# Second product of the routed experts: two fp32 matmuls replaced by five fp32r passes over weights and hidden channels split in two parts

## The chip, the cores and the metric

The kernel runs on one core of a Trainium2 chip. The metric is the device time of one execution in microseconds (us). Engines are named as in the profile: PE (TensorE matmul), PEld (its weight loads), DVE (VectorE), ACT (ScalarE), POOL (GpSimd), SP (SyncE, which issues most of the DMAs).

## The reference, cut to what matters

The block is FFN, attention, FFN over 1024 tokens of width 256. Both FFNs use the same weights. The FFN has a shared expert and 16 routed experts of which each token takes four:

```
q_weights, ids = top_k(softmax(x @ gate_w.T), 4)
for each expert e:                      # w13_e: 352 x 256, w2_e: 256 x 176
    h   = silu(x @ w13_e[:176].T) * (x @ w13_e[176:].T)     # 176 hidden channels
    acc = acc + (h @ w2_e.T) * coef_e
out = shared(x) + acc
x   = x + 0.5 * ffn(layernorm(x))       # then attention, then the same FFN again
```

The change concerns `h @ w2_e.T`, the second product, with 176 channels as the contraction.

## The kernel before

Each engine has its own instruction list, written out by hand, and semaphores order them. A layer (an FFN) runs in three stages.

First, norm and router, and 9 of 12 "units" of the shared expert (PE lines 399, 404, 422: fp32 matmuls). Meanwhile POOL scatters rows of the normed tokens to a DRAM area sorted by expert (L853, 32 indirect DMAs a layer), and ACT and DVE split the first expert weights `w13`. ACT copies a float32 weight to fp32r (`WH`, L741) and DVE subtracts that from the weight (`WL`, L966), so `WH + WL` is the weight. `PARTED` says after which unit which experts are split. In the second layer `w13` is loaded again and only `WL` is computed again.

Second, the slots: 47 tiles (`TL`) of 128 token rows, each of one expert whose number is read from a table in SBUF by each engine (`values_load`, TENSOR_LOAD in the trace). An iteration i of the loop holds, on PE: the first product of tile i (L449 to L453, six fp32r passes of 352 columns: hidden token part times WH and WL, lower token part `xl` times WH), the two transposes of the rows of tile i+1 (L434), the second product of tile i-2 (L474, two fp32 matmuls of 256 columns, 88 channels each), and the two transposes of the hidden values of tile i-1 (L461). ACT: silu(i) (L719), the upper part `xt` of tile i+1 (L714), the result of tile i-2 (L725). DVE: row numbers (L1068) and the hidden values `hm` of tile i (L1072), TENSOR_LOAD (L1062), the lower part `xl` of tile i+1 (L1084), a copy `ht` of the transposed hidden values of tile i-1 (L1078). POOL scatters the result rows (L860). Each engine takes its list in that order, and a wait in it holds everything behind it.

Third, the last three shared units, and the gathered result rows are added.

SP issues all input loads in one order: x, constants, shared weights, `w13` in four parts (L313), `W2` (L314), then the slot rows (L332) once all scatters have landed.

## Time and profile before

| | |
|---|---|
| device time, median of 3 runs | 477.45 us (475.16 to 477.74) |
| device time of the profiled execution | 481.29 us |
| its span | 479.5 us |
| PE busy / PEld busy | 440.3 us (92%) / 336.8 us (70%) |
| DVE / ACT / POOL busy | 277.9 (58%) / 168.4 (35%) / 197.9 us (41%) |
| chain of waits, share by engine | PE 82%, DVE 12%, ACT 2%, issue 2% |
| costliest PE group | L474, x376, 97.9 us, mean 382 ns |

Busy time counts overlapping matmuls once. A matmul's own duration is longer than its distance to the next one, since they are pipelined: a cost on PE is read from start to start. Where a list waits on a semaphore, the wait hangs on the next instruction of the list.

### The profile page before, as it was taken

The numbers are of one execution on the slowest core, as the hardware profiler recorded it, in microseconds if no ns is written. First come the engines' busy times: TensorE is split into PE (matmuls) and PEld (weight loads), VectorE is DVE, ScalarE is ACT, GpSimd is POOL, SyncE is SP. The second block draws the span as 40 slices with busy tenths as digits, with TensorE's granted clock in tenths as the row PEclk, the third lists the DMA queues.
The fourth block names the chain that finished last, engine by engine and source line by source line (L and its number), as shares of the span: only waits on it lengthen the run. The fifth ranks groups of instructions, "written<-read, shape, count | busy, mean of one in ns | idle before, by whom it ended". The sixth has DMA issues, their size and how long they took to land.

```text
span 479.5 us, 8311 instructions
## 1 busy us (share of the span) xinstructions
PE 440.3 (92%) x2151; PEld 336.8 (70%) x2151; DVE 277.9 (58%) x801; ACT 168.4 (35%) x466; POOL 197.9 (41%) x207
## 2 busy tenths in 40 slices
PE   6889998999999998989979879899899999999890
PEld 4545567998999995534679755455699899999550
DVE  5664665655665562494876444667565566556237
ACT  3221632444444441227556312010244444444210
POOL 0177720444344443630354107785044444444462
PEclk9988998999999998989989768999999999999895
DMA  7999731344344422900000097322334444442192
GB/s 257 385 390 329 244 111 51 118 126 123 123 124 125 121 81 71 411 1 2 0 0 1 2 333 255 117 86 96 90 118 127 121 126 122 125 122 92 56 350 88
DMA packets 40219, 67.35 MB, mean 140 GB/s; under 512 B 5040, under 2 KB 31408, under 8 KB 40176
## 3 DMA queue, kind: packets, MB, share of 16 engines
q1 hardware_dynamic: 32592, 45.05, 29.2%
q0 software_dynamic: 7584, 21.77, 12.9%
q8 instruction: 21, 0.34, 0.3%
q14 instruction: 22, 0.18, 0.1%
HBM read 41.64 MB, written 25.17 MB: 139 GB/s over the span
## 4 chain that ended last, share of the span: by engine, by line
PE 82%; DVE 12%; ACT 2%; issue 2%; DMA 1%; DVEq 0%; ACTq 0%
PE ps L474 17%; PE ps L399 9%; PE ps L422 8%; PE ps L404 7%; PE ps L453 7%; PE ps L449 7%; PE ps L450 6%; PE ps L434 4%; PE ps L461 4%; PE ps L539 3%; DVE X L1101 2%; PE ps L368 2%; PE ps L620 2%; PE ps L355 1%; DVE WR L1100 1%
## 5 line engine op out<-in xcount | busy, mean ns | idle before, releaser
L860 POOL DMA_INDIRECT rows<-ar,idx x94 | 90.3, 960 | 155.5 <-ACT ar L725 152.7
L474 PE MATMUL ps<-W,ar 88*128 x376 | 97.9, 382 | 2.8 <-DVE ar L1078 2.8
L853 POOL DMA_INDIRECT slots<-XR,pos x64 | 67.5, 1055 | 59.3 <-DVE pos L1026 40.4
L1072 DVE SCALAR_TENSOR_TENSOR ar<-ps,XR,ar 128x176 f32<-128x176 f32 x94 | 37.7, 401 | 84.1 <-ACT ar L719 84.1
L449 PE MATMUL ps<-WH,xt 128*128 x188 | 69.3, 369 | 2.8 <-ACT xt L714 1.5
L474 PEld LDWEIGHTS ps<-W,ar 88*128 88x128 f32 x376 | 63.9, 190 | 9.1 <-issue 3.8
L450 PE MATMUL ps<-WL,xt 128*128 x188 | 61.0, 325 | 0.0
L719 ACT ACTIVATE ar<-ps 128x176 f32<-128x176 f32 x94 | 29.9, 318 | 81.8 <-PE ps L453 81.8
L725 ACT ACTIVATE ar<-ps 128x256 f32<-128x256 f32 x94 | 36.2, 385 | 50.8 <-PE ps L474 50.8
L399 PE MATMUL ps<-XT,WS 128*128 128x512 f32 x96 | 52.8, 679 | 1.0 <-ACT sgt L702 1.0
L422 PE MATMUL ps<-WS,ar 128*128 128x256 f32 (+1 forms) x192 | 46.0, 385 | 4.1 <-DVE ar L954 4.1
L422 PEld LDWEIGHTS ps<-WS,ar 128*128 128x128 f32 (+1 forms) x192 | 36.0, 190 | 19.6 <-issue 9.3
L453 PE MATMUL ps<-WH,xl 128*128 x188 | 46.3, 327 | 0.5 <-DVE xl L1084 0.3
L708 ACT ACTIVATE ar<-ps 128x512 f32<-128x512 f32 (+1 forms) x24 | 14.3, 596 | 86.7 <-PE ps L399 86.7
L1084 DVE TENSOR_TENSOR xl<-ps,xt 128x256 fp32r<-128x256 f32 x94 | 39.9, 424 | 6.9 <-issue 3.1
L1078 DVE COPY ar<-ps 88x256 f32<-88x256 f32 x94 | 39.5, 420 | 3.7 <-PE ps L461 3.7
L714 ACT ACTIVATE xt<-ps 128x256 fp32r<-128x256 f32 x94 | 36.1, 384 | 10.1 <-PE ps L434 10.0
L404 PE MATMUL ps<-XT,WS 128*128 128x512 f32 x80 | 39.4, 616 | 0.0
L449 PEld LDWEIGHTS ps<-WH,xt 128*128 128x128 f32 x188 | 35.6, 189 | 4.4 <-issue 4.4
L461 PE MATMUL ps<-cst,ar 128*88 128x128 f32 x188 | 36.3, 274 | 0.0
L434 PE MATMUL ps<-cst,XR 128*128 128x128 f32 x188 | 36.0, 273 | 0.0
L450 PEld LDWEIGHTS ps<-WL,xt 128*128 128x128 f32 x188 | 36.0, 192 | 0.0
(151 smaller groups left out, 596.4 us busy)
## 6 DMA issues: line engine op xcount, KB each, us to landing
XR<-slots SPq DMA_DIRECT2D x94, 144.0 KB, 2.1
WR<-w SPq DMA_DIRECT2D x8, 1408.0 KB, 14.6
WR<-rows SPq DMA_DIRECT2D x16, 512.0 KB, 7.1
W<-w SPq DMA_DIRECT2D x1, 3072.0 KB, 28.7
slots<-zeros SPq DMA_DIRECT2D x1, 2304.0 KB, 12.8
rows<-ar,idx POOLq DMA_INDIRECT x94
X<-x SPq DMA_DIRECT2D x4, 256.0 KB, 4.3
WS<-wsh SPq DMA_DIRECT2D x2, 512.0 KB, 7.8
```

Of the source, the lines that this page charges most:

```text
L399: mm = pe.matmul(ps[:, 4 + u % 2, :], WS1[:, k, 2 * j, :], XT[:, k, half(h)], start=k == 0, stop=k == KD - 1)
L404: mm = pe.matmul(ps[:, 6 + u % 2, :], WS1[:, k, 2 * j + 1, :], XT[:, k, half(h)], start=k == 0, stop=k == KD - 1)
L422: mm = pe.matmul(ps[:, 2 * h + i // 2, i % 2 * D:(i % 2 + 1) * D], Hs[u % 2][rows, tok(i)], WS2[rows, j, :], start=first and i % 2 == 0, s ...
L434: mm = pe.transpose(ps[:, i % 2, k * P:(k + 1) * P], xs[i % NX][:, k * P:(k + 1) * P], ident)
L449: pe.matmul(to, token, WH[:, bass.ds(e, 1), k, :].rearrange("p a n -> p (a n)"), start=k == 0, stop=False)
L450: pe.matmul(to, token, WL[:, bass.ds(e, 1), k, :].rearrange("p a n -> p (a n)"), start=False, stop=False)
L453: mm = pe.matmul(to, xl[i % 2][:, k * P:(k + 1) * P], WH[:, bass.ds(e, 1), k, :].rearrange("p a n -> p (a n)"), start=False, stop=k == KD - 1)
L461: mm = pe.transpose(ps[0:KE, 6 + i % 2, c * P:(c + 1) * P], hm[i % 2][:, c * KE:(c + 1) * KE], ident)
L474: mm = pe.matmul(ps[:, 2 + i % 2, 0:D], ht[i % 2][:, c * P:(c + 1) * P], w, start=c == 0, stop=c == 1)
L853: pool.indirect_dma_start(out=slots_dram[:, :], out_offset=bass.IndirectOffsetOnAxis(ap=pos[:, t, r:r + 1], axis=0), in_=XR[:, t, :], in_o ...
L860: pool.indirect_dma_start(out=rows_dram[:, :], out_offset=bass.IndirectOffsetOnAxis(ap=idx[:, i:i + 1], axis=0), in_=ys[i % NY], in_offset ...
L1084: dve.tensor_tensor(xl[i % 2], ps[:, i % 2, 0:D], xt[i % 2].bitcast(F32), ALU.subtract).then_inc(s_xl, 1)
```

## The change

The weights of the second product are kept as three fp32r arrays. Of the 176 channels the first 112 (`FM`) are the main part, the last 64 (`FR`) the rest. `MH` and `ML` are the upper and lower part of the main weights (112 partitions). `RH` holds the upper part of the rest in partitions 0 to 63 and its lower part in 64 to 127. DVE writes the hidden values with the rest twice (a tile of 112 + 64 + 64), so that the second transpose has the rest in both halves of the partitions. ACT makes the upper part `hh` of the transposed values, DVE the lower part `hl`, and PE makes five fp32r passes: hh x MH, hh x ML, hh x RH (upper and lower weights at once), hl x MH, hl x RH (upper only). The arrays are made once, in the first layer's units 2, 3 (rest) and 7, 8 (main). The rest is loaded twice ahead of `w13`; the main weights are loaded into the same buffer once the rest is split. The DMA descriptor scratch per partition is set to 2048 bytes.

```
-PARTED = {3: (0, 2), ... 8: (14, NE)}
+W2_FIRST = {2: (0, 8), 3: (8, NE)}
+W2_LAST = {7: (0, 4), 8: (4, NE)}
 # SP
+            for b in range(2):
+                sp.dma_start(MR[b * FR:(b + 1) * FR, :, :], w2r).then_inc(s_w2r, 16)
             for e in range(0, NE, 4):
                 sp.dma_start(WR[:, e:e + 4, :, :], w13[e:e + 4]...)
-            sp.dma_start(W2[:, :, :, :], w2.rearrange("e c p n -> p e c n")).then_inc(s_w2, 16)
+            sp.wait_ge(s_rl, len(W2_FIRST))
+            sp.wait_ge(s_rh, len(W2_FIRST))
+            sp.dma_start(MR[0:FM, :, :], w2m).then_inc(s_w2m, 16)
 # PE, slot_hidden
-                wait(pe, s_htc, TL * f + i - 1)
-                for c in range(2):
-                    mm = pe.transpose(ps[0:KE, 6 + i % 2, c * P:(c + 1) * P], hm[i % 2][:, c * KE:(c + 1) * KE], ident)
+                wait(pe, s_hl, TL * f + i - 1)
+                pe.transpose(ps[0:FM, 6 + i % 2, 0:P], hm[i % 2][:, 0:FM], ident)
+                pe.transpose(ps[:, 6 + i % 2, P:2 * P], hm[i % 2][:, FM:FM + P], ident).then_inc(s_ht, 1)
 # PE, slot_out
-                pe.wait_ge(s_htc, TL * f + i + 1)
-                for c in range(2):
-                    w = W2[0:KE, bass.ds(e, 1), c, :]...
-                    mm = pe.matmul(ps[:, 2 + i % 2, 0:D], ht[i % 2][:, c * P:(c + 1) * P], w, start=c == 0, stop=c == 1)
+                pe.wait_ge(s_hh, TL * f + i + 1)
+                pe.matmul(to, hh[i % 2][main, 0:P], of(MH, main), start=True, stop=False)
+                pe.matmul(to, hh[i % 2][main, 0:P], of(ML, main), start=False, stop=False)
+                pe.matmul(to, hh[i % 2][:, P:2 * P], of(RH, slice(0, P)), start=False, stop=False)
+                pe.wait_ge(s_hl, TL * f + i + 1)
+                pe.matmul(to, hl[i % 2][main, 0:P], of(MH, main), start=False, stop=False)
+                pe.matmul(to, hl[i % 2][rest, P:2 * P], of(RH, rest), start=False, stop=True).then_inc(s_l2, 1)
 # ACT, slots: last of an iteration
+                def hidden(i):
+                    act.wait_ge(s_ht, TL * f + i + 1)
+                    wait(act, s_l2, TL * f + i - 1)
+                    act.activation(hh[i % 2], ps[:, 6 + i % 2, 0:D], ACT.Copy).then_inc(s_hh, 1)
 # ACT, part(u), ahead of the WH copies
+                if u in W2_FIRST:
+                    act.activation(RH[:, some, :], MR[:, some, :], ACT.Copy).then_inc(s_rh, 1)
+                if u in W2_LAST:
+                    act.activation(MH[:, some, :], MR[0:FM, some, :], ACT.Copy).then_inc(s_mh, 1)
 # DVE, part(f, u), first layer, ahead of the WL subtractions
+                    dve.tensor_tensor(RH[FR:P, some, :], MR[FR:P, some, :], RH[FR:P, some, :]..., ALU.subtract)
+                    dve.tensor_tensor(ML[:, some, :], MR[0:FM, some, :], MH[:, some, :]..., ALU.subtract)
 # DVE, slots
-                    dve.scalar_tensor_tensor(hm[i % 2], ps[:, 4 + i % 2, FE:2 * FE], row[:, bass.ds(e + R_CF, 1)], sg[i % 2], ...)
+                    dve.scalar_tensor_tensor(hm[i % 2][:, 0:FM], ps[:, 4 + i % 2, FE:FE + FM], rate, sg[i % 2][:, 0:FM], ...)
+                    twice = hm[i % 2][:, FM:FM + 2 * FR].rearrange("p (a n) -> p a n", a=2)
+                    dve.scalar_tensor_tensor(twice, spread(ps[:, 4 + i % 2, FE + FM:2 * FE], 1, 2), rate, spread(sg[i % 2][:, FM:FE], 1, 2), ...)
-                    dve.tensor_copy(ht[i % 2], ps[0:KE, 6 + i % 2, 0:D]).then_inc(s_htc, 1)
+                    dve.tensor_tensor(hl[i % 2][0:FM, :], ps[0:FM, 6 + i % 2, 0:D], hh[i % 2][0:FM, :]..., ALU.subtract).then_inc(s_hl, 1)
-    nc = bacc.Bacc("TRN2", target_bir_lowering=False, num_devices=1)
+    nc = bacc.Bacc("TRN2", target_bir_lowering=False, num_devices=1, dynamic_dma_scratch_size=2048)
```

(`PARTED` itself stays as it was.)

On PE, in the first iteration of the slots that has all four parts, before: the second row transpose, the second product (`W` is the array W2, `ar` holds ht), then the hidden transposes.

```order
L434 MATMUL ps<-cst,XR 128x128
L474 ISA [waits s_htc,s_xsh,s_w2]
L474 MATMUL ps<-W,ar 128x256
L474 ISA
L474 MATMUL ps<-W,ar 128x256
L478 TENSOR_LOAD tab
L461 MATMUL ps<-cst,ar 88x128 [waits s_hm]
L461 MATMUL ps<-cst,ar 88x128
```

The same place now:

```order
L449 MATMUL ps<-cst,XR 128x128
L492 ISA [waits s_hh,s_xsh,s_ml]
L492 MATMUL ps<-MH,hh 128x256
L493 REGISTER_ALU
L493 MATMUL ps<-ML,hh 128x256
L494 REGISTER_ALU
L494 MATMUL ps<-RH,hh 128x256
L496 MATMUL ps<-MH,hl 128x256 [waits s_hl]
L497 MATMUL ps<-RH,hl 128x256
L500 TENSOR_LOAD tab
L475 MATMUL ps<-cst,ar 112x128 [waits s_hm]
L476 MATMUL ps<-cst,ar 128x128
```

Two matmuls became five with two waits among them, where one wait on the copy stood; nothing else changed its place on PE.

On DVE, one iteration of the slots before (`idx` row numbers, `ar` first hm and then ht):

```order
L1068 ISA [waits s_xs3]
L1068 SCALAR_TENSOR_TENSOR idx<-XR,valid,spare 128x1
L1072 ISA [waits s_ht,s_sil]
L1072 SCALAR_TENSOR_TENSOR ar<-ps,XR,ar 128x176
L1062 TENSOR_LOAD tab
L1084 TENSOR_TENSOR xl<-ps,xt 128x256 [waits s_l1,s_xtc]
L1078 COPY ar<-ps 88x256 [waits s_l2,s_ht]
```

and now:

```order
L1112 ISA [waits s_xs3]
L1112 SCALAR_TENSOR_TENSOR idx<-XR,valid,spare 128x1
L1117 ISA [waits s_ht,s_sil]
L1117 SCALAR_TENSOR_TENSOR ar<-ps,XR,ar 128x112
L1121 SCALAR_TENSOR_TENSOR ar<-ps,XR,ar 128x128
L1106 TENSOR_LOAD tab
L1134 TENSOR_TENSOR xl<-ps,xt 128x256 [waits s_l1,s_xtc]
L1127 TENSOR_TENSOR hl<-ps,hh 112x256 [waits s_l2,s_hh]
```

A second SCALAR_TENSOR_TENSOR stands between the silu's wait and the subtraction `xl`, and the copy became a subtraction that waits for ACT in place of PE.

## Rows read from the trace of the kernel before

**Rows 1.** Busy time by engine, clock and DMA in the slots of the first layer.

```profile
core 0: us, PE busy (x) PEld busy (x) DVE busy (x) ACT busy (x) POOL busy (x), PEclk, DMA share, GB/s
90.00:180.00 90.00, 89.91 (x554) 81.97 (x553) 53.16 (x159) 38.95 (x119) 37.45 (x39) 1.00 0.39 117
```

**Rows 2.** Timeline of PE, one steady iteration: start us, us, engine, line, tiles.

```profile
152.92 0.49 PE L453 MATMUL ps<-WH,xl 128*128 x2
...
155.04 0.32 PE L450 MATMUL ps<-WL,xt 128*128 x1
155.20 0.48 PE L453 MATMUL ps<-WH,xl 128*128 x2
155.52 0.38 PE L434 MATMUL ps<-cst,XR 128*128 128x128 f32 x2
155.73 1.03 PE L474 MATMUL ps<-W,ar 88*128 x4
156.60 0.38 PE L461 MATMUL ps<-cst,ar 128*88 128x128 f32 x2
```

**Rows 3.** Timeline, second layer, tiles 1 to 2, where no second product stands yet.

```profile
343.53 0.30 PEld L453 LDWEIGHTS ps<-WH,xl 128*128 128x128 f32 x2
343.64 0.48 PE L453 MATMUL ps<-WH,xl 128*128 x2
...
344.09 0.21 PEld L461 LDWEIGHTS ps<-cst,ar 128*88 128x88 f32 x2
344.16 0.32 ACT L719 ACTIVATE ar<-ps 128x176 f32<-128x176 f32 x1 [1.41 <-PE ps L453]
...
344.62 0.40 DVE L1072 SCALAR_TENSOR_TENSOR ar<-ps,XR,ar 128x176 f32<-128x176 f32 x1 [1.01 <-ACT ar L719]
...
344.90 0.42 PE L449 MATMUL ps<-WH,xt 128*128 x1 [0.34 <-ACT xt L714]
...
345.06 0.42 DVE L1084 TENSOR_TENSOR xl<-ps,xt 128x256 fp32r<-128x256 f32 x1
...
345.54 0.30 PEld L453 LDWEIGHTS ps<-WH,xl 128*128 128x128 f32 x2
345.64 0.49 PE L453 MATMUL ps<-WH,xl 128*128 x2
```

**Rows 4.** The table reads of DVE's and PE's sequencers: duration ns min/median/max.

```profile
L1062 DVEq TENSOR_LOAD <-tab x94: 299/306/570, 73.0 to 444.8; - x94
```

```profile
L478 PEldq TENSOR_LOAD <-tab x94: 295/301/529, 69.7 to 444.2; - x94
```

**Rows 5.** Groups by line: busy us, mean ns of one, idle before it.

```profile
L1072 DVE SCALAR_TENSOR_TENSOR ar<-ps,XR,ar 128x176 f32<-128x176 f32 x94 | 37.7, 401 | 84.1 <-ACT ar L719 84.1
...
L1173 DVE SCALAR_TENSOR_TENSOR U<-U,G,ps 128x128 f32<-128x128 f32 x12 | 3.6, 340 | 0.0
```

**Rows 6.** Timeline of DVE in attention: two such instructions, back to back.

```profile
246.42 0.60 DVE L1173 SCALAR_TENSOR_TENSOR U<-U,G,ps 128x128 f32<-128x128 f32 x2
```

**Rows 7.** Timeline of DVE in the first layer's unit 3.

```profile
44.38 0.69 DVE L954 TENSOR_TENSOR ar<-ps,ar 128x512 f32<-128x512 f32 x1 [2.54 <-PE ps L404]
```

**Rows 8.** Timeline of ACT and DVE, first layer, from unit 8 to the slots.

```profile
67.58 1.46 ACT L741 ACTIVATE WH<-WR 128x704 fp32r<-128x704 f32 x2
```

```profile
69.47 1.68 DVE L966 TENSOR_TENSOR WL<-WR,WH 128x704 fp32r<-128x704 f32 x2
72.26 1.66 DVE L969 SCALAR_TENSOR_TENSOR X<-ps,gate,X 128x256 f32<-128x256 f32 x4 [1.10 <-PE ps L422]
73.83 0.41 DVE L1084 TENSOR_TENSOR xl<-ps,xt 128x256 fp32r<-128x256 f32 x1
```

**Rows 9.** Timeline of PE at the end of the first layer's slots.

```profile
180.18 0.49 PE L453 MATMUL ps<-WH,xl 128*128 x2
...
184.51 1.65 PE L474 MATMUL ps<-W,ar 88*128 x4 [0.71 <-DVE ar L1078]
185.96 3.09 PE L399 MATMUL ps<-XT,WS 128*128 128x512 f32 x4
```

**Rows 10.** The DMAs: DMA share while weights load, SP's long wait, POOL's scatters.

```profile
55.00:60.00 5.00, 5.00 (x17) 2.54 (x15) 3.62 (x6) 3.19 (x5) 4.05 (x4) 1.00 0.39 139
```

```profile
SPq L327 <- DMA slots<-XR,pos: 32.1, 1, 32.1
```

```profile
L853 POOL DMA_INDIRECT slots<-XR,pos x64 | 67.5, 1055 | 59.3 <-DVE pos L1026 40.4
```

```profile
DMA to landing us min/median/max: 2.4/3.0/7.0
```

More of the change, by code:

```diff
@@ L62, in spread, with macaron @@
     return a.broadcast_to(shape)
-def macaron(nc, x, w13, w2, wsh1, wsh2, wgate, wkqv, woT, normw, consts, out):
+def macaron(nc, x, w13, w2m, w2r, wsh1, wsh2, wgate, wkqv, woT, normw, consts, out):
     ctx = ExitStack()
@@ L101, in aside @@
             return a
-        W2 = sb("W2", [KR, NE, 2, D])
+        RH = sb("RH", [P, NE, D], F32R)
+        MH = sb("MH", [FM, NE, D], F32R)
+        with nc.sbuf_tensor("ML", [FM, NE, D], F32R) as ML:
+            pass
+        MR = sb("MR", [P, NE, D])
         WS1 = sb("WS1", [P, KD, 2 * NJ - 1, P])
@@ L159, in macaron @@
             with nc.sbuf_tensor("xl", [P, 2, D], F32R) as xl_all:
-                pass
+                with nc.sbuf_tensor("hh", [P, 2, D], F32R) as hh_all:
+                    with nc.sbuf_tensor("hl", [P, 2, D], F32R) as hl_all:
+                        pass
         xt = [xt_all[:, h, :] for h in range(2)]
         xl = [xl_all[:, h, :] for h in range(2)]
+        hh = [hh_all[:, h, :] for h in range(2)]
+        hl = [hl_all[:, h, :] for h in range(2)]
         ar = sb("ar", [P, 6 * N])
@@ L171, in macaron @@
         sg = [area(3072 + h * FE, FE) for h in range(2)]
-        hm = [area(3072 + (2 + h) * FE, FE) for h in range(2)]
-        ht = [ar[0:KE, 4480 + h * D:4480 + (h + 1) * D] for h in range(2)]
+        hm = [area(3424 + h * (FM + 2 * FR), FM + 2 * FR) for h in range(2)]
         xs = [XR[:, i, :] for i in range(NX)]
@@ L214, in macaron @@
         s_x = [sem(f"s_x{q}") for q in range(4)]
-        s_cst, s_wg, s_ws, s_ws2, s_w2, s_wa, s_fill, s_out = (
-            sem(n) for n in "s_cst s_wg s_ws s_ws2 s_w2 s_wa s_fill s_out".split())
+        s_cst, s_wg, s_ws, s_ws2, s_wa, s_fill, s_out = (
+            sem(n) for n in "s_cst s_wg s_ws s_ws2 s_wa s_fill s_out".split())
         s_we = [sem(f"s_we{q}") for q in range(NE // 4)]
         s_wh, s_wl, s_xl = (sem(n) for n in "s_wh s_wl s_xl".split())
+        s_w2r, s_rh, s_rl, s_w2m, s_mh, s_ml = (sem(n) for n in "s_w2r s_rh s_rl s_w2m s_mh s_ml".split())
         s_set = sem("s_set")
@@ L224, in macaron @@
         s_xs = [sem(f"s_xs{i}") for i in range(NX)]
-        s_tx, s_xtc, s_l1, s_sil, s_hm, s_ht, s_htc, s_l2, s_y = (
-            sem(n) for n in "s_tx s_xtc s_l1 s_sil s_hm s_ht s_htc s_l2 s_y".split())
+        s_tx, s_xtc, s_l1, s_sil, s_hm, s_ht, s_hh, s_hl, s_l2, s_y = (
+            sem(n) for n in "s_tx s_xtc s_l1 s_sil s_hm s_ht s_hh s_hl s_l2 s_y".split())
         s_st = [sem(f"s_st{b}") for b in range(NY)]
@@ L734, in slots @@
                         result(i - 2)
+                    if 1 <= i <= TL:
+                        hidden(i - 1)
             def part(u):
+                if u in W2_FIRST:
+                    act.wait_ge(s_w2r, 32)
+                    some = slice(*W2_FIRST[u])
+                    act.activation(RH[:, some, :], MR[:, some, :], ACT.Copy).then_inc(s_rh, 1)
+                if u in W2_LAST:
+                    act.wait_ge(s_w2m, 16)
+                    some = slice(*W2_LAST[u])
+                    act.activation(MH[:, some, :], MR[0:FM, some, :], ACT.Copy).then_inc(s_mh, 1)
                 for e in range(*PARTED.get(u, (0, 0))):
@@ L959, in part @@
             def part(f, u):
+                if f == 0 and u in W2_FIRST:
+                    dve.wait_ge(s_rh, list(W2_FIRST).index(u) + 1)
+                    some = slice(*W2_FIRST[u])
+                    dve.tensor_tensor(RH[FR:P, some, :], MR[FR:P, some, :], RH[FR:P, some, :].bitcast(F32), ALU.subtract).then_inc(s_rl, 1)
+                if f == 0 and u in W2_LAST:
+                    dve.wait_ge(s_mh, list(W2_LAST).index(u) + 1)
+                    some = slice(*W2_LAST[u])
+                    dve.tensor_tensor(ML[:, some, :], MR[0:FM, some, :], MH[:, some, :].bitcast(F32), ALU.subtract).then_inc(s_ml, 1)
                 for e in range(*PARTED.get(u, (0, 0))):
@@ L1095, in slots @@
                     if 1 <= i <= TL:
-                        turned(i - 1)
+                        rest(i - 1)
             def combine(f, t):
```

27 lines of the change are left out of this document (17 added, 10 removed).

## The prediction

> **What bounds the kernel now.** I read the shares of the chain of waits first: PE carries 82% of it, and its costliest group is the one that the change replaces. The question is whether PE stays the bound once that group shrinks. The stretches by engine come next: in the slots PE is busy 89.91 of 90 us at a granted clock of 1.00, the higher level (2.4 GHz), DVE 53.16 and ACT 38.95 [rows 1]. Then the timeline of one iteration. Between the two L453 pairs lie 2.28 us [rows 2]. The first product's six passes start 0.16 apart, the two row transposes take 0.21 (155.52 to 155.73), the second product 0.87 (155.73 to 156.60), the hidden transposes some 0.22. Nothing there waits. The 12 iterations from 152.92 to the last L453 at 180.18 [rows 9] take 2.27 each.
>
> The row that matters most is found where the second product is missing, in the second layer's first tiles [rows 3]. PE has 0.87 us less to do there, and yet its period is 345.64 - 343.64 = 2.00, not 1.41: it waits for `xt` (344.90, idle 0.34), and the weight load of L453 comes at 345.54, 0.06 after `xl` ends (345.06 + 0.42 = 345.48). That shows a loop through three engines. Counted from the end of one `xl`, E = 343.48: load at +0.05, matmul +0.16, silu +0.68, L1072 +1.14, then 0.44 to L1084, which takes 0.42, so the next E comes at +2.00. Written out, the loop is 1.56 + s, where s is the time from the start of the hidden values on DVE to the start of `xl`, now 0.44. At a period of 2.27 it has 0.27 of slack. The change takes from PE and adds to s.
>
> **The change, part by part.**
>
> PE. The second product goes: -0.87. Five passes of 256 columns come. No row has an fp32r pass of 256 columns. From above it is the 0.16 of 352 columns [rows 2]; from below the 0.107 or so at which transposes with 128-column weight loads follow each other (0.21 for two). I take 0.12 (the 352-column pitch less 96 columns at 2.4 GHz, 0.04), near the transposes, and the range is 0.107 to 0.16. Five are 0.60 (0.54 to 0.80). The hidden transposes have 112 and 128 columns of weights in place of 88 and 88; the row transposes with 128 cost 0.21, so nothing is added. PE's own period becomes 2.27 - 0.87 + 0.60 = 2.00 (1.94 to 2.20). Its sequencer has more to issue behind the wait for `xl`: in rows 3 it went from the load at 343.53 to that of L461 at 344.09, 0.56 us for four matmuls with their loads and a TENSOR_LOAD of 0.30 [rows 4]. That is at most 0.26 for eight instructions; ten more and three register instructions add some 0.45, so the load of the hidden transposes is reached after 1.0, while the array gets there after 0.16 + 0.32 + 0.21 + 0.60 = 1.29. Hidden, with 0.3 to spare.
>
> DVE, inside the loop. One instruction of 176 columns becomes two, 112 and 128. Two of 128 in a row take 0.60, one 0.34, so they start 0.26 apart [rows 5, 6]. By the difference of 401 and 340 ns over 48 columns, 112 columns are some 0.02 shorter. Now `xl` can start once both are in, at 0.24 + 0.26 = 0.50, and once the table read is through. The read takes 0.306 [rows 4] of today's s of 0.44, and stands one instruction later, so some 0.50 too. I take s = 0.52. From below it is 0.44 (all hidden under the read), from above 0.84 (0.44 and a whole further instruction of 0.40). The loop becomes 1.56 + 0.52 = 2.08 (2.00 to 2.40). That is longer than PE's 2.00: after the change PE waits for `xl` in each iteration, about 0.08, and the bound has moved from PE to the loop.
>
> Here a rule of the Trainium skill speaks against the change. "VectorE: DVE Perf Modes", section "The TRN2 errata — SBUF-src ops pay a fixed extra latency per instruction", has a fixed term of 151 cycles in each fp32 tensor_tensor, (N + 151)/0.96 ns. By it the split adds 0.157 for the second instruction and 0.067 for 64 more columns, so s = 0.66 and the loop 2.22, an estimate. The trace disagrees in part, as part of the fixed term overlaps the next instruction: durations of 0.34 start 0.26 apart [rows 6].
>
> DVE and ACT, outside the loop. The copy of 0.42 becomes a subtraction of about the same size, as L1084 with 0.42 shows [rows 3]. It waits for `hh` of ACT, an extra 0.38 on an ACT that is 43% busy [rows 1]. From the end of `xl` counted: hidden transposes end at +1.3 + 0.38, `hh` by +2.2, `hl` by +2.75. The next iteration needs `hh` at 2.08 + 0.70 and `hl` in its fourth pass at 2.08 + 1.05 = 3.13: 0.4 early. DVE has 53.16/90 of 2.27 = 1.34 busy in an iteration, and 0.2 more fits in 2.08. If that cover went, PE would lose what `hl` is late, one for one.
>
> Slots. With 42 steady iterations in the first layer and 44 in the second: 86 x (2.27 - 2.08) = -16.3. DVE's table read is sometimes 0.57 in place of 0.306 [rows 4], which the slack of 0.27 hides now and will not then; a few such reads, +0.5.
>
> Start of the slots, first layer. After unit 8 ACT first copies the main weights of 12 experts, 3072 columns. Two copies of 704 take 1.46 [rows 8]: 3.2 in proportion, 2.7 if the fixed part is paid once. From 67.58 that ends at 70.3. DVE then subtracts 3072 columns (two of 704 take 1.68: 3.4 with the fixed part once) to 73.8, then its two `WL` (1.68) to 75.5, the four shared sums (73.83 - 72.26 = 1.57) to 77.05, and only then `xl` of tile 0, which stands at 73.83 now: +3.2. PE idles there some 3 us and its clock may stay at the lower level (1.2 GHz) for an iteration more, +0.5. Together +3.7 (2.5 to 6).
>
> The other preparations are covered. In units 2 and 3 DVE gains 2.4 each (2048 columns); it is idle 2.54 before unit 3 [rows 7], and unit 3 is followed by more idle time. The rest weights are loaded ahead of `w13`, 2.1 MB, and delay it some 6 to 7 us; experts are split no sooner than 43 us. The main weights are issued after unit 3's subtraction, about 47.5; the queues that drained by 55 to 60 (DMA share 0.39 [rows 10]) carry 0.8 MB more, some 3 us, so the load lands near 60, and its first copy follows the silu of unit 7, about 62.4. If it were late, unit 8 would move one for one beyond some 1 us. SP's new wait stands ahead of the slot rows, which wait for the scatters 32.1 us anyway [rows 10].
>
> End of the slots. From the last L453 to the first unit lie 5.78 us [rows 9]. Two of the three second products stand alone there behind a chain transpose, copy, product. The chain gets ACT's copy in front of the subtraction (+0.5 each), but the first three passes run under the subtraction, so only two follow it (0.22 and the load, for 0.87, at half clock 1.45 in the last). I get 4.5 to 5.5: -0.8 a layer, -1.6 (-2.4 to 0).
>
> Sum: -16.3 + 0.5 + 3.7 - 1.6 = -13.7. On the profiled execution's 481.29 that is 467.6; the median of the runs shown is 3.8 lower, so 477.45 - 13.7 = 463.8.
>
> **Rivals.**
> A. The fixed cost counts: the second instruction adds its whole 0.26, less 0.02 to 0.07, after today's 0.44 (s = 0.63 to 0.68, loop 2.19 to 2.24), or a pass costs the 0.16 of the wider ones (PE 2.20). For it: no row shows either piece alone. Against: overlap in rows 6. At 2.21, 86 x 0.06 = -5.2, with +3.7 - 1.6 that is -3.1: 474.4. The page's rule above comes out here too.
> B. The read hides both instructions and the loop stays at 2.00: 86 x 0.27 = -23.2, + 2.1 = -21.1, 456.4. Against: 0.50 of input is more than 0.44.
> C. Slower: the loop on DVE eats more than PE gives. If the doubled, broadcast second instruction holds `xl` back by a whole 0.40 (s = 0.84), the period is 2.40: 86 x 0.13 = +11.2, + 2.1 = +13.3, 490.7. It decides from s = 0.69 (period 2.25) on. For it: what is removed is paid on PE and what is added stands in the one place of DVE that the loop passes.
> D. The smaller descriptor scratch holds POOL up. Scatters now start 1.27 to 1.35 apart (1055 ns and (59.3 - 40.4)/62 = 0.30) and land after 2.4 to 7.0 us [rows 10], so up to six are in flight. If it held one, each would take 3.0 + 0.96, in 64 scatters +170. If it holds six or more, nothing. No row shows its size in scatters. By the Trainium skill, "DMA: Bandwidth & Descriptors", sections "Terms" and "The descriptor swizzle", a descriptor is 16 bytes and an engine gets 9 each way for a 128-partition transfer; 2048 bytes would hold 14 transfers, an estimate that no run here shows.
>
> **How the numbers follow.** Forecast 0.60 (loop 2.05 to 2.14, 461 to 469), A 0.16, B 0.08, C 0.13, D 0.03. Changes within 0.5% (2.4 us) are no change as far as a measurement tells. Faster: 0.60, B, and most of A, 0.78. Same: A with a costlier start, 0.07. Slower: C with D, 0.15. The range 457 to 476 leaves out C, D and some of B.
>
> **What would show it.** The slots' period 2.08 (start of L453 to start of L453), a PE idle of under 0.1 before it put down to DVE `xl`; five passes 0.12 apart; two hidden instructions 0.24 apart and `xl` 0.52 after the first; the first `xl` of layer one at about 77. It is wrong if the period is above 2.15, if PE waits for `hl`, or if POOL's scatters come more than 1.4 apart.

## The result, and the profile after

| | median us | runs | ratio to before, 95% interval |
|---|---|---|---|
| before | 476.52 (475.16 to 477.74) | 4 | 1 |
| after | 498.27 (497.76 to 501.54) | 4 | 1.0472 [1.0415, 1.0528] |

The forecast was 463.8; the result is 21.8 us slower than before and 34.5 over the forecast. The profiled execution of after took 498.18 with a span of 496.4. Two executions of kernels in the experiments, of 545.58 and 1408.28 us, lay far above the others of their kernels and are left out of the ratios.

PE still carries the chain of waits (79%, before 82%). It is busy for 439.6 us, before 440.3: a smaller share of a longer span (89%, before 92%), but no less work, although the second product was meant to get cheaper. So it was not VectorE's loop that took PE's place.

Milestones of both traces, before and now: the first row transposes of the first layer (L434, now L449) start at 72.06 and 83.94, the last at 178.24 and 193.19, so the slots take 3.07 more. The next unit starts at 185.96 [rows 9] and 200.57, so the tail from the last transposes takes 0.34 less. In layer two the way from the table's cast on DVE to the first transposes takes 32.89 and 34.49, and the slots take 104.27 and 106.84. Together the starts give +13.5 where +3.7 was forecast, and the slots +5.6 where -16.3 was.

The slots first. The window that answers to [rows 1]:

```profile
90.00:180.00 90.00, 89.86 (x574) 78.42 (x573) 56.18 (x191) 51.61 (x153) 35.46 (x37) 0.99 0.39 117
```

PE has 89.86 of 90 us again, at nearly the same clock (0.99, before 1.00). One iteration on PE, as [rows 2] (start us, duration us):

```profile
176.84 0.38 PE L449 MATMUL ps<-cst,XR 128*128 128x128 f32 x2
176.98 0.36 PE L492 MATMUL ps<-MH,hh 112*128 x1
177.18 0.28 PE L493 MATMUL ps<-ML,hh 112*128 x1
177.30 0.28 PE L494 MATMUL ps<-RH,hh 128*128 x1
177.42 0.28 PE L496 MATMUL ps<-MH,hl 112*128 x1
177.63 0.38 PE L497 MATMUL ps<-RH,hl 64*128 x1
177.94 0.32 PE L475 MATMUL ps<-cst,ar 128*112 128x128 f32 x1
178.10 0.27 PE L476 MATMUL ps<-cst,ar 128*128 128x128 f32 x1
...
179.18 0.38 PE L449 MATMUL ps<-cst,XR 128*128 128x128 f32 x2
```

The period (called pitch below: from one tile's row transposes to the next tile's) is 2.34, and nothing waits. Passes of 112 and 128 rows follow 0.12 apart, as forecast. L497, on 64 rows, comes 0.21 after its neighbour, and what follows it 0.31 later. The weight loads show where the time goes (timeline of PE's loads, another iteration):

```profile
153.83 0.19 PEld L494 LDWEIGHTS ps<-RH,hh 128*128 128x128 f32 x1
153.94 0.19 PEld L496 LDWEIGHTS ps<-MH,hl 112*128 112x128 f32 x1
154.28 0.18 PEld L497 LDWEIGHTS ps<-RH,hl 64*128 64x128 f32 x1
154.59 0.13 PEld L475 LDWEIGHTS ps<-cst,ar 128*112 128x112 f32 x1
154.64 0.14 PEld L476 LDWEIGHTS ps<-cst,ar 128*128 128x128 f32 x1
```

Other loads start 0.11 after the one before, ahead of their matmul. The loads at 154.28 and 154.59 start together with their matmul: neither runs ahead of the matmul before it, at the change to 64 rows or back. From the fourth pass (L496) to the next first product (L464) lie 0.72 us, and 0.43 in the run with 128 rows below: the change costs 0.29.

Then the start of layer one. GpSimd's scatters come first (in the bracket its idle time before, and what ended it), then VectorE:

```profile
37.47 0.96 POOL L890 DMA_INDIRECT slots<-XR,pos  x1 [0.30 <-issue]
43.59 1.68 POOL L890 DMA_INDIRECT slots<-XR,pos  x1 [5.15 <-issue]
45.57 2.73 POOL L890 DMA_INDIRECT slots<-XR,pos  x1 [0.30 <-issue]
...
70.44 5.24 POOL L890 DMA_INDIRECT slots<-XR,pos  x1 [2.18 <-issue]
75.98 0.96 POOL L890 DMA_INDIRECT slots<-XR,pos  x1 [0.30 <-issue]
...
78.51 0.96 POOL L890 DMA_INDIRECT slots<-XR,pos  x1 [0.30 <-issue]
```

```profile
69.87 3.36 DVE L1004 TENSOR_TENSOR ML<-MR,MH 112x3072 fp32r<-112x3072 f32 x1 [0.82 <-ACT MH L773]
73.14 1.69 DVE L1010 TENSOR_TENSOR WL<-WR,WH 128x704 fp32r<-128x704 f32 x2
74.75 1.65 DVE L1013 SCALAR_TENSOR_TENSOR X<-ps,gate,X 128x256 f32<-128x256 f32 x4
```

Two things delay the scatters. GpSimd stops after the 14th (5.15 us) and after 14 more (2.18). And a scatter lasts 5.24 in place of 0.96 while VectorE subtracts. The last one ends at 79.47, before at 63.34. SP loads the slot rows only once all scatters have landed. In this run and in those below whose last scatter ends at 68 or later, the first transposes come 4.4 to 4.5 us behind its end, so there the scatters set the start. Before, they had 8.7 us. VectorE's own row is as forecast: free at 76.4 for `xl` (forecast 77). But the slot rows aren't there, and PE idles from 72 to 84 and starts at a granted clock of 0.50, the lower level (1.2 GHz):

```profile
75.00:85.00 10.00, 0.66 (x2) 0.29 (x2) 1.40 (x4) 0.36 (x1) 3.56 (x4) 0.50 0.31 101
85.00:90.00 5.00, 4.22 (x14) 3.76 (x15) 1.69 (x6) 0.72 (x3) 0.00 (x0) 0.50 0.42 112
```

### The profile page after: what moved, and what is told of

The parts are those of the page before. It is cut to its first block, busy times and chain, and to the rows that moved or that the text cites. A ratio compares the mean times of both kernels' runs of the same rounds, so it can differ in the third digit from the quotient of the medians.

```text
span 496.4 us, 8884 instructions
## 1 busy us (share of the span) xinstructions
PE 439.6 (89%) x2245; PEld 330.1 (66%) x2245; DVE 303.5 (61%) x899; ACT 209.2 (42%) x564; POOL 208.7 (42%) x207
## 3 DMA queue, kind: packets, MB, share of 16 engines
q0 software_dynamic: 7584, 21.77, 12.4%
## 4 chain that ended last, share of the span: by engine, by line
PE 79%; DVE 12%; issue 5%; ACT 3%; DMA 1%; DVEq 0%; ACTq 0%
PE ps L414 9%; PE ps L437 7%; PE ps L464 7%; PE ps L419 6%; PE ps L468 6%; PE ps L465 6%; PE ps L497 6%; PE ps L475 5%; PE ps L449 4%; PE ps L561 3%; PE ps L492 2%; PE ps L494 2%; PE ps L496 2%; PE ps L493 2%; PE ps L476 2%
## 5 line engine op out<-in xcount | busy, mean ns | idle before, releaser
L890 POOL DMA_INDIRECT slots<-XR,pos x64 | 78.2, 1221 | 66.4 <-issue 46.0
L464 PE MATMUL ps<-WH,xt 128*128 x188 | 69.6, 371 | 2.8 <-ACT xt L736 2.7
L1127 DVE TENSOR_TENSOR hl<-ps,hh 112x256 fp32r<-112x256 f32 x94 | 39.9, 424 | 38.0 <-ACT hh L752 33.9
L1117 DVE SCALAR_TENSOR_TENSOR ar<-ps,XR,ar 128x112 f32<-128x112 f32 x94 | 31.3, 333 | 49.5 <-ACT ar L741 49.5
L414 PE MATMUL ps<-XT,WS 128*128 128x512 f32 x96 | 51.3, 661 | 1.0 <-ACT sgt L724 1.0
L449 PE MATMUL ps<-cst,XR 128*128 128x128 f32 x188 | 36.5, 276 | 13.7 <-issue 13.7
L468 PE MATMUL ps<-WH,xl 128*128 x188 | 46.6, 329 | 0.0
L1134 DVE TENSOR_TENSOR xl<-ps,xt 128x256 fp32r<-128x256 f32 x94 | 38.8, 413 | 11.6 <-ACT xt L736 8.7
L736 ACT ACTIVATE xt<-ps 128x256 fp32r<-128x256 f32 x94 | 36.1, 384 | 21.8 <-PE ps L449 21.6
L464 PEld LDWEIGHTS ps<-WH,xt 128*128 128x128 f32 x188 | 36.0, 191 | 4.7 <-issue 4.7
L419 PE MATMUL ps<-XT,WS 128*128 128x512 f32 x80 | 38.5, 604 | 0.0
L449 PEld LDWEIGHTS ps<-cst,XR 128*128 128x128 f32 x188 | 26.5, 142 | 16.6 <-issue 14.5
L492 PE MATMUL ps<-MH,hh 112*128 x94 | 33.9, 361 | 2.8 <-ACT hh L752 2.8
L752 ACT ACTIVATE hh<-ps 128x256 fp32r<-128x256 f32 x94 | 36.2, 385 | 0.0
```

The lines of the kernel that those rows point to most:

```text
L414: mm = pe.matmul(ps[:, 4 + u % 2, :], WS1[:, k, 2 * j, :], XT[:, k, half(h)], start=k == 0, stop=k == KD - 1)
L419: mm = pe.matmul(ps[:, 6 + u % 2, :], WS1[:, k, 2 * j + 1, :], XT[:, k, half(h)], start=k == 0, stop=k == KD - 1)
L449: mm = pe.transpose(ps[:, i % 2, k * P:(k + 1) * P], xs[i % NX][:, k * P:(k + 1) * P], ident)
L464: pe.matmul(to, token, WH[:, bass.ds(e, 1), k, :].rearrange("p a n -> p (a n)"), start=k == 0, stop=False)
L468: mm = pe.matmul(to, xl[i % 2][:, k * P:(k + 1) * P], WH[:, bass.ds(e, 1), k, :].rearrange("p a n -> p (a n)"), start=False, stop=k == KD - 1)
L492: pe.matmul(to, hh[i % 2][main, 0:P], of(MH, main), start=True, stop=False)
```

## The experiments

The experiments ran on five chips, each time with the kernel before beside them on the same chip, so times from different chips are compared by their ratios to it. On two of the chips it took 477.21 and 479.05; on three others 528.35, 527.83 and 528.3, which has a part of its own below.

### The slots: the 64-row pass and VectorE's loop

**128 rows in the fifth pass** (`hl` computed on 128 partitions):

```diff
-  pe.matmul(to, hl[i % 2][rest, P:2 * P], of(RH, rest), start=False, stop=True)
+  pe.matmul(to, hl[i % 2][:, P:2 * P], of(RH, slice(0, P)), start=False, stop=True)
```

> The changed kernel with one thing altered: the fifth pass of the second product (lower parts of the last 64 channels) runs over all 128 partitions in place of 64; the lower parts are computed on 128 partitions, and the pass adds a product of lower by lower parts. The theory that the change of row count costs the time: in the trace after, the 64-row pass begins with its weight load (154.28 and 154.28), 0.31 us before the next load, where passes of 112 and 128 rows follow 0.12 apart; so PE's period falls from 2.335 us by some 0.29 to the 2.05 to 2.08 of the loop through DVE, 86 slots give 22 to 25 us, and the time is 475.5 (473 to 478). The profile shows loads at 0.12 for all five passes. The rival, that the slots are held by the loop through ScalarE and VectorE or by the wait for the lower parts: the period stays at 2.3 and the time at 498. A second rival, that it is the number of passes (a cost of each fp32r pass): the same 498.

Measured: 475.47, ratio 0.9966 [0.9939, 0.9993], on the forecast. One iteration:

```profile
153.43 0.38 PE L449 MATMUL ps<-cst,XR 128*128 128x128 f32 x2
...
154.00 0.28 PE L496 MATMUL ps<-MH,hl 112*128 x1
154.12 0.28 PE L497 MATMUL ps<-RH,hl 128*128 x1
154.24 0.27 PE L475 MATMUL ps<-cst,ar 128*112 128x128 f32 x1
...
155.51 0.38 PE L449 MATMUL ps<-cst,XR 128*128 128x128 f32 x2
```

All follow 0.12 apart, and the pitch of the slots is 2.07. More arithmetic made the pass cheaper. The tails got shorter too: from the last L468 (before L453) to the next unit 4.58 and 4.78 us in the two layers, where the changed kernel has 5.37 and 5.51 and the kernel before 5.78 and 5.45.

**The kernel before, split in 112 and 64 rows** (`ROWS` is (112, 64)):

```diff
-  mm = pe.matmul(ps[:, 2 + i % 2, 0:D], ht[i % 2][:, c * P:(c + 1) * P], w, ...)
+  mm = pe.matmul(ps[:, 2 + i % 2, 0:D], ht[i % 2][0:ROWS[c], c * P:(c + 1) * P], w, ...)
```

> The kernel before with its contraction of 176 channels split in 112 and 64 rows in place of 88 and 88; both products stay fp32. The theory that a matmul of 64 rows between others of more rows costs some 0.29 us on PE whatever the type (in the trace before a unit of 64 rows had 1.92 us to the next one where others had 1.73): the period of a slot rises from 2.27 to 2.46 or 2.56, 86 slots give 16 to 25 us, and the time is 493 to 502. The rival, that it lies in the fp32r passes alone: 476.5 (475 to 478).

The two hidden transposes change with it, from 88 and 88 columns to 112 and 64. Measured: 512.63, ratio 1.0701 [1.0643, 1.076], and a pitch of 2.61. The cost is there in fp32 too, and somewhat larger: 0.34. Its loads are idle 0.33 on either side of the 64 rows:

```profile
151.51 0.30 PEld L475 LDWEIGHTS ps<-W,ar 112*128 112x128 f32 x2
152.14 0.29 PEld L475 LDWEIGHTS ps<-W,ar 64*128 64x128 f32 x2 [0.33 <-issue]
152.77 0.17 PEld L462 LDWEIGHTS ps<-cst,ar 128*112 128x112 f32 x2 [0.33 <-DVE ar L1073]
```

**The 64-row pass twice** (after, L497 issued a second time):

> The changed kernel with its 64-row pass issued twice (its small term is counted twice in the result). If the cost of 0.29 us lies in the change to a matmul of 64 rows and back, the second adds 0.12 and the pitch of the slots goes from 2.335 to 2.45, the time from 498 to 508. If each matmul of 64 rows pays it, the second adds 0.25 to 0.3, the pitch is 2.6 and the time 521. If the loop through VectorE holds the slots, neither: 498.

Measured: pitch 2.45, ratio 1.0779 [1.0718, 1.0841] (515.57, two runs beside 479.05). The second pass adds 0.11. So the cost is the change into 64 rows and out again, once each, not the pass. The ratio lies 3.1% over that of after, 14.7 us, and the pitch gives 9.9 of them. In the profiled executions the two tails take 2.0 more, and the stretch from the next unit to layer two's slots 159.0 for 153.8, at a mean granted clock of 0.90 for 0.96. The lower clock goes with that stretch being longer; why it was lower isn't shown.

```profile
152.30 0.18 PEld L497 LDWEIGHTS ps<-RH,hl 64*128 64x128 f32 x1
152.41 0.19 PEld L498 LDWEIGHTS ps<-RH,hl 64*128 64x128 f32 x1
152.72 0.13 PEld L475 LDWEIGHTS ps<-cst,ar 128*112 128x112 f32 x1
```

**96 rows in the fifth pass** (after with `hl` and `RH` cut to 0:96):

> The changed kernel with the fifth pass over 96 partitions (2048 bytes of scratch; a part of the lower by lower product is added). If what costs is that a matmul of 64 rows uses half of the array, 96 rows follow at 0.12 as 112 and 128 do: pitch 2.07, 475.5. If any pass that is shorter than its neighbours pays, the pitch is 2.33 and the time 498.

Measured: 484.13 where the kernel before took 527.83, 0.9163 [0.91, 0.9226]; the pitch is 2.07, and it can be compared across chips: the changed kernel has 2.34 on a chip of either kind. A pass of 96 rows between 112 and 128 costs nothing extra.

**VectorE's hidden values in one instruction** (the second copy isn't written from tile 2 on), first run and a second:

```diff
-  dve.scalar_tensor_tensor(hm[:, 0:FM], ...)    
-  dve.scalar_tensor_tensor(twice, ...)      
+  dve.scalar_tensor_tensor(hm[:, 0:FE], ...)
```

> As the kernel with the fifth pass over 128 partitions and the scratch at 4864 bytes, but from the third tile of each layer on VectorE makes the hidden values in one instruction of 176 columns: the second copy of the last 64 channels isn't written (the partitions 64 to 127 hold old values, so the products with the lower parts of those channels are left out of the result). If the loop through VectorE (1.56 us and the time from the first hidden values to the lower parts, 0.51) sets the period of 2.065, that time falls to some 0.26 and the period to TensorE's own sum: 2.00, and 86 times 0.065 are 5.6 us less. If TensorE's own sum is the 2.065, the time stays within 1 us.

> The kernel with 128 rows in the fifth pass, 4864 bytes, and the hidden values of all tiles but the first two of each layer in one instruction (the second copy of the last 64 channels left out) once more. In its first run the pitch of the slots fell from 2.07 to 2.02. By the theory that the loop through VectorE set the 2.07, and TensorE's own sum the 2.02: 86 times 0.05 are 4 us under the 465.9 of the kernel with both instructions: 461.5 (460 to 463). The rival, that the slots are set by TensorE alone: 466.

Measured: 517.06 beside 520.74 of the kernel with both instructions, and 516.17; both on chips where the kernel before takes 528 (0.9781 [0.974, 0.9823] and 0.977 [0.9711, 0.9829]). The median pitch was 2.02 both times, 2.07 with two instructions.

```profile
121.53 0.40 DVE L1125 SCALAR_TENSOR_TENSOR ar<-ps,XR,ar 128x176 f32<-128x176 f32 x1 [0.46 <-ACT ar L741]
121.98 0.42 DVE L1138 TENSOR_TENSOR xl<-ps,xt 128x256 fp32r<-128x256 f32 x1
...
123.55 0.40 DVE L1125 SCALAR_TENSOR_TENSOR ar<-ps,XR,ar 128x176 f32<-128x176 f32 x1 [0.41 <-ACT ar L741]
```

Here s is 0.45, not the expected 0.26: the one instruction takes 0.40 itself. The period is 2.02. With two instructions in the run with 128 rows s was 0.51 (154.08 to 154.59) and the period 2.07. Both are 1.56 + s to 0.01. Less work on VectorE alone shortened the period, so at 2.07 the loop is the bound; at 2.02 it can be the loop (2.01) or PE's own sum (forecast 2.00), and no run parts them.

### The start: GpSimd's scatters

**The kernel before with 2048 bytes of scratch**:

```diff
-  nc = bacc.Bacc("TRN2", target_bir_lowering=False, num_devices=1)
+  nc = bacc.Bacc("TRN2", target_bir_lowering=False, num_devices=1, dynamic_dma_scratch_size=2048)
```

> The kernel before with the scratch for DMA descriptors at 2048 bytes a partition and nothing else. The theory that the scratch stops GpSimd until it has drained: a stretch of 2 to 5 us without work after 14 and after 28 scatters, the last one 4 to 7 us later than at 63.3; since the first second product waited for other things until 74.3, a part of it is hidden: 479.5 (477.5 to 482). The rival, that it costs nothing without the added subtractions on VectorE: 476.5 and no idle stretch.

Measured: 486.12, ratio 1.0167 [1.0122, 1.0212], more than expected. The stops stand after 14 and 28 scatters:

```profile
46.09 1.14 POOL L853 DMA_INDIRECT slots<-XR,pos  x1 [6.65 <-issue]
...
67.91 0.97 POOL L853 DMA_INDIRECT slots<-XR,pos  x1 [2.18 <-issue]
```

The first transposes come 5.4 later, the first four tiles take 12.0 in place of 10.3 with more of them at the lower clock, and layer two starts 1.6 later: 8.7 together. I had left out the last two.

**After with 4608 bytes**:

> The changed kernel with the scratch for DMA descriptors at 4608 bytes a partition in place of 2048 (32 scatters in place of 14). The theory that the full scratch holds GpSimd: its idle stretches of 5.15 us after 14 scatters and of 2.18 after 28 go, the last scatter of layer 1 ends near 72 in place of 79.5, the first second product of layer 1 near 79 in place of 86.6, and layer 2 gives some 1.5 us at its start: 488 (485 to 491). The rival, that VectorE's subtractions with both inputs in SBUF hold GpSimd's scatters by themselves (records of 2.7 to 5.2 us) and that they only start sooner: the last scatter still ends after 76, where these subtractions end, and the time is 494 to 498.

Measured: 494.65, ratio 1.0341 [1.0284, 1.0399]; the first transposes at 81.0. The stop after 14 is gone. But one of 2.35 stands before the 32nd scatter, and pushes it into the subtractions, here 71.47 to 76.51 beside `ML` and `WL`, which end at 75.68. The two delays feed each other. The stop moves with the size, from the 15th scatter to the 32nd, and with 4864 bytes below there is none: it is the scratch that stops GpSimd. By the Trainium skill, "DMA: Bandwidth & Descriptors", sections "Terms" and "The descriptor swizzle", a descriptor has 16 bytes and a transfer to 128 partitions has 9 on each side of an engine, which makes 144 bytes a scatter, an estimate: 14.2 of them in 2048, and 32 in 4608. The traces agree, but for one scatter: 14 and 31 ran without a stop.

**128 rows and 4864 bytes**, and once more on a chip with 479:

> The changed kernel with the fifth pass over 128 partitions and the scratch for DMA descriptors at 4864 bytes a partition (33 scatters of 144 bytes in place of 14; with 4608 the 32nd still waited 2.35 us, and then met VectorE's subtractions for 5.04). The theory of both stalls (full scratch, and the last scatters pushed into the subtractions): no idle stretch on GpSimd, the last scatter ends near 71, the first transposes of layer 1 come near 76 to 78 in place of 83.9, fewer tiles run at the lower clock, layer 2 gives 1.6 us: 475.5 - 6 - 1 - 1.6 = 467 (464 to 469.5). The rival, that the subtractions hold GpSimd whenever its scatters fall: the last one ends after 75, the first transposes after 80: 470 to 473.

> The kernel with the fifth pass over 128 partitions and 4864 bytes of scratch once more, since in its first run the chip held VectorE for 27 us until 65.5 (every kernel there took some 50 us longer), so its scatters ended before any subtraction began. Where the subtractions fall beside the scatters again: by the theory of both stalls the last scatter ends near 71 and the first transposes come at 76 to 78, 467 (464 to 469.5) where the kernel before takes 477; by the rival, that the subtractions hold GpSimd wherever its scatters fall, 470 to 473.

Measured: 520.74 (0.9853 [0.9806, 0.9901], before at 528.35), where the scatters ended at 62 and no subtraction met them; then 465.93, ratio 0.9741 [0.9704, 0.9777]. GpSimd never stops, the last scatter ends at 69.90, and VectorE's row of work is what the first `xl` waits for, at the time that the prediction gave:

```profile
75.11 1.66 DVE L1013 SCALAR_TENSOR_TENSOR X<-ps,gate,X 128x256 f32<-128x256 f32 x4
76.68 0.42 DVE L1134 TENSOR_TENSOR xl<-ps,xt 128x256 fp32r<-128x256 f32 x1
```

**Copies in place of the second weights' subtractions** (4608 bytes, one input in place of two; the arrays of lower parts then hold the whole weights, so the result isn't the reference's), twice:

> The changed kernel with the scratch at 4608 bytes, in which VectorE copies the second weights (one input in SBUF) where it subtracted their upper parts (two inputs in SBUF); the subtractions for the first weights stay. The lower parts of the second weights are then wrong by their upper parts, so the output isn't the reference's. The theory that an instruction with both inputs in SBUF holds GpSimd's scatters: the records of 2.62 and 2.74 us at 43 to 49 fall to 0.96 to 1.4, those of 3.86 and 5.04 at the end get shorter by what the copy is shorter, the first transposes come 2 to 4 us sooner than at 81.0: 491 to 493. The rival, that any long instruction of VectorE does it, or that the scatters were slow by themselves: the records stay at 2.6 and 2.7, and the time at 494.5.

> The kernel with copies of the second weights (one input) in place of their subtractions (two inputs) once more, 4608 bytes of scratch, output not the reference's. By the theory that an instruction with both inputs in SBUF holds GpSimd: the scatters beside the two copies at 43 to 49 take 0.96 to 1.4 us (2.62 and 2.74 beside the subtractions), and those beside the subtractions of the first weights are still prolonged. By the rival (any long instruction of VectorE): they take 2.6 and 2.7 or as long as the copy is.

Measured: 536.19 (1.0132 [1.0078, 1.0187], before at 528.35), where scatters and copies did not meet; then 486.26 (two runs), 1.0166 [1.0108, 1.0225]. My theory, that it takes two inputs in SBUF, fell. VectorE and GpSimd in the second:

```profile
41.20 1.35 DVE L1000 CAST RH<-MR 64x2048 fp32r<-64x2048 f32 x1
...
43.56 1.22 DVE L1000 CAST RH<-MR 64x2048 fp32r<-64x2048 f32 x1
```

```profile
41.83 1.55 POOL L890 DMA_INDIRECT slots<-XR,pos  x1 [0.31 <-issue]
43.68 1.94 POOL L890 DMA_INDIRECT slots<-XR,pos  x1 [0.30 <-issue]
```

The scatters end 0.83 and 0.84 behind the copies, as in the other runs behind the subtractions (69.11 behind 68.28, 76.51 behind 75.68 with 4608 bytes). So one input holds them as two do. What had a PSUM input did not: in the run with 4608 bytes four shared sums ran from 75.59 while that scatter finished. The gain of 8 us on that run, more than I had expected, came since the last scatter, at 67.05, now got ahead of the last group, which starts at 68.82.

By the Trainium skill, "SBUF — State Buffer", section "SBUF: two separate sides", VectorE holds the port pair that it shares with GpSimd for a whole instruction in a two-port mode, an fp32 copy within SBUF among them (here they are casts to fp32r), and GpSimd can't write its DMAs' descriptors meanwhile. The traces agree for the copies. For instructions with two SBUF inputs the page has the lock only against a GpSimd operation that reads SBUF. The scatters were held by those too; they take their row numbers from `pos`, an array in SBUF, and no run tells whether that is why.

The kernel before is not free of it. Its `WL` subtractions hold scatters as well, mostly for 0.3 us each, and one for longer, 0.83 behind the third of three:

```profile
319.87 3.71 POOL L853 DMA_INDIRECT slots<-XR,pos  x1 [0.30 <-issue]
320.27 2.48 DVE L966 TENSOR_TENSOR WL<-WR,WH 128x704 fp32r<-128x704 f32 x3
```

The change added longer instructions to it, and the stops of the scratch pushed scatters into them.

**Lower parts of experts 4 to 15 moved behind the first `xl`** (128 rows, 4864 bytes), three runs:

```diff
   left(0)
+  late(0)
 ...
+  if i == 0:
+      late(1)
```

> The kernel of the last run with the lower parts of the second weights for experts 4 to 15 moved: ScalarE makes their upper parts after its last unit, VectorE subtracts them between its first values of the slots, and TensorE waits for all three groups ahead of the first second product. The theory that VectorE's row of subtractions (3.36 us for 3072 elements) sets the start of the slots once the scatters are in time: the first transposes come 2 to 3 us sooner, 464 (461.5 to 466). The rival, that the start is set by the landing of the last scatters: no change from the last run. A second rival: the moved subtractions (3.4 us) only delay the first tiles by as much, no change or 1 us more.

> The kernel with the moved lower parts of the second weights once more, for the same reason. In its first run it stood 9 us under the kernel that it was derived from. By the theory that VectorE's row of subtractions sets the start of the slots: 2.5 to 4 us under the run beside it, 463 (460.5 to 465.5); by the rival, that the landing of the last scatters sets it, the same as the run beside it. What I hold for likelier is the first.

> The kernel with the moved lower parts beside the next two, as their base and for a second profile: 462.4 (461 to 464) where the kernel before takes 477 to 479. The profile of its last run, taken at the upper end of its times, did not show where it gains 3.5 us on the one without the move: the first lower parts of the inputs came 1.7 us sooner, but the slots ended only 0.3 sooner, since more tiles ran at the lower clock. By the theory that the start is what the move gains, a profile near the median shows fewer tiles at the lower clock and the slots' end 2 us sooner.

Measured: 511.79, 0.9701 [0.9656, 0.9745] (before at 528.35); **462.4, 0.9657 [0.9616, 0.9699]** (before at 479.05), the fastest kernel of the study; 511.37, 0.9678 [0.962, 0.9735] (before at 527.83). On the chip with 479 that is 3.5 under the kernel without the move, as expected. On the chip with 528.35 it is 9 under (511.79 and 520.74). Where the 3.5 lie isn't shown: the profiled execution, 465.84, was the slowest of its kernel, `xl` came at 75.01 for 76.68, but the slots began with more tiles at the lower clock and ended 0.3 sooner only.

**Subtractions in pieces of 512 elements**, first with 4864 bytes, then with 2048:

```diff
-  dve.tensor_tensor(RH[FR:P, some, :], ...)
+  for k in range(a, b, 2):
+      ins = dve.tensor_tensor(RH[FR:P, k:k + 2, :], ...)
```

> The kernel with the moved lower parts, in which VectorE's subtractions of the second weights ahead of the slots are cut into pieces of 512 elements (12 in place of 3). In the traces so far a scatter that began inside one of them ended 0.83 to 0.84 us behind its end, while pieces of 704 elements at 50 to 61 prolonged scatters to no more than 1.6. The theory that one instruction holds GpSimd until its own end: the records of 2.45, 2.74 and 3.37 us fall to 1.6 or less, the last scatter ends near 66 in place of 69.5, VectorE's first xl comes when its sums are done, at 73.4 in place of 75.0, and the time falls by 1 to 2 us. The rival, that instructions back to back hold it as one (a record of 3.85 spanned ML and three WL): the records and the time stay.

> The kernel with 128 rows in the fifth pass, the moved lower parts and the subtractions in pieces of 512 elements, but with the 2048 bytes of scratch of the changed kernel, so that its scatters fall beside the subtractions on any chip. The theory that one long instruction holds GpSimd until its own end: the scatters beside the lower parts of the second weights (2.73, 1.42 and 3.39 us in the run with 128 rows and nothing moved) take 1.6 or less, the one of 5.23 near 70 is gone with the moved group, the two stalls of the full scratch stay (5.2 and 2.2), the last scatter ends at 71 to 72.5 in place of 79.4, and the time is 468 (465 to 471) where the kernel before takes 477. The rival (instructions back to back hold it as one): records of 2.7 and 3.4 stay, only the moved group shows, the last scatter ends near 75, 471 to 472. On a chip on which the kernel before takes 528, where a kernel with 2048 bytes took 484.1 and ones with 4864 took 511 to 521: 477 (473 to 480), if what costs there goes with the size of the scratch.

Measured: 512.83, 0.9704 [0.9654, 0.9754], beside 511.37 for its base; the scatters ended at 61.91, ahead of all subtractions, so it tells nothing. Then 480.8, 0.9118 [0.9072, 0.9164], where the kernel before took 528.3; the execution in the profile took 472.73. Beside eight pieces of `RH` (44.14 to 46.64 and 47.40 to 49.96) no scatter is long, but one beside three `WL` is:

```profile
45.98 1.50 POOL L895 DMA_INDIRECT slots<-XR,pos  x1 [0.31 <-issue]
47.79 1.14 POOL L895 DMA_INDIRECT slots<-XR,pos  x1 [0.30 <-issue]
...
67.56 3.35 POOL L895 DMA_INDIRECT slots<-XR,pos  x1 [2.95 <-issue]
```

So pieces do help (2.73 before at the same place), but a row of short ones (67.57 to 70.06) can still hold a scatter to its end, here 0.85 behind it. Other traces have both cases too. In the trace after, a scatter at 54.60 ended 0.83 behind the first `WL` of a row of three, though the next had begun; one at 64.87 was held through three of them. The kernel before has the first case at 59.17 and the second at 319.87. What decides between them stays open.

### The same kernels on other chips

> The changed kernel as it is, once more. On a chip on which the kernel before takes 477: 498. On one on which it takes 528: since the kernel before has 16384 bytes of scratch and waits there for an unknown queue some 50 us in all, and the one with 2048 bytes and 96 rows in the fifth pass 8.6 us, the changed kernel takes 484.1 + 22.4 = 506.5 (504 to 510) and is faster than the kernel before by 4%. The rival, that the queue's waits belong to something else that differs: 545.

Measured: 514.33, ratio 0.9721 [0.9658, 0.9785]: where the kernel before takes 528.3, the changed kernel is 2.8% **faster**. The direction was expected, the size not (506.5). In the run with moved lower parts and 4864 bytes ScalarE and VectorE both stop in mid-layer for something that the profile doesn't name (`remote`). It begins while the DMA engines are full (share 1.05) and lasts beyond the last scatter's end at 61.84:

```profile
66.69 0.60 ACT L731 ACTIVATE ar<-ps 128x512 f32<-128x512 f32 x1 [30.65 <-remote]
```

```profile
63.15 0.26 DVE L1103 CAST tab<-ps 128x94 int32<-128x94 f32 x1 [24.30 <-remote]
```

```profile
40.00:45.00 5.00, 4.99 (x12) 3.86 (x13) 0.00 (x0) 0.00 (x0) 3.78 (x5) 0.57 1.05 389
```

With 2048 bytes ScalarE's longest such wait was 11.4 and 12.9 us (96 rows, and the changed kernel). The cleanest pair is the kernel with pieces, whose two runs differ in the scratch alone: 512.83 with 4864 bytes and 480.8 with 2048, on two such chips that give the kernel before within 0.5 us of each other. That is 32 us for the smaller scratch, which on the other two chips costs 10.8 (the step between 2048 and 4864 bytes with 128 rows). So the size of the scratch matters there, and the other way round. What the engines wait for is not shown. Nor is whether it belongs to the chip or to the time at which it ran, since each chip was used at one time only. No trace of the kernel before was taken on such a chip, nor was it run there with 2048 bytes: that its 528 are such waits is argued from the others.

## Why the prediction was wrong

Its failed step is "Five are 0.60 (0.54 to 0.80)": the PE term. The distance of 0.12 was right for four passes. The fifth goes to 64 rows and back and costs 0.29 more, so PE's own period is 2.34 in place of 2.00. That is 86 x (2.335 - 2.08) = 21.9 us of the 34.5 missed, shown by the run with 128 rows (-22.8 between the medians, 24 by the ratios) and by the repeated pass. The trace before had the sign: the unit of 64 rows there has 1.92 us to its successor where one of 128 rows takes 1.73 (54.46 - 52.73). I bounded the pass from rows of 128 partitions alone.

```profile
52.73 1.89 PE L422 MATMUL ps<-WS,ar 128*128 128x256 f32 x8
54.46 1.88 PE L399 MATMUL ps<-XT,WS 128*128 128x512 f32 x4
...
57.98 1.99 PE L422 MATMUL ps<-WS,ar 64*128 64x256 f32 x8
59.90 1.98 PE L399 MATMUL ps<-XT,WS 128*128 128x512 f32 x4
```

By the Trainium skill, "TensorE: Matmul & The Clock Gate", section "Step-by-step: what each phase is for", the time of a weight load goes by its columns, and the row count doesn't matter for it. The traces agree for the load itself: 0.18 us with 64 rows, 0.19 with 112 and 128. What costs is that this load and the next start later, which the load's own time doesn't show.

The second failed step is in rival D: "If it holds six or more, nothing." It holds 14, and yet it cost: after 14 of them GpSimd stopped for 5.15 us and then ran 14 more, so it isn't freed scatter by scatter; after 28 it stopped for 2.18. And the start counted VectorE's new subtractions on VectorE only, not what they do to GpSimd. The starts came out at +13.5 for +3.7. In the run with 128 rows and 4864 bytes, without stops and with the last scatter ahead of the last group of subtractions, the first transposes come at 74.31 for 83.94 and layer two starts 1.6 sooner. That step is 2.25% of the time, 10.8 us. How it divides between the stops and the held scatters isn't shown: each brings on the other.

What held: s = 0.52 (measured 0.51), the loop as 1.56 + s (2.07 when PE is no longer above it), hence a bound that would have moved to VectorE; two hidden instructions 0.25 apart; `hl` never waited for; the first `xl` at 77 as far as VectorE goes (76.68). The tails gave -0.35 together in place of -1.6, by the same pass: with 128 rows in it they give -1.9. With both faults taken out the kernel stands at -12.4 us (interval -14.2 to -10.7) where the sum was -13.7. Rival C and the first half of A put a loss on VectorE, and no run shows it there. The second half of A had PE at 2.20, by wider distances between all passes; four of the five are 0.12 apart, so it was near in number and not in cause. The page's rule that would have made s 0.66 is not borne out: 0.51.

## What to carry over

Price a matmul by its row count against its neighbours': between passes of 96 to 128 rows one of 64 cost 0.29 to 0.34 us for the change in and out, and padding it to 128 rows was free. A smaller descriptor scratch cost a stop of 2 us or more each time it filled, and long VectorE instructions within SBUF held GpSimd's scatters: count both when a change takes memory or adds preparation ahead of a scatter's reader. And time a kernel on more than one chip; the verdict here turned, from 4.7% slower to 2.8% faster.
